# Scores of the state-space scan: sixteen 64x64 products a chunk become eight products with 64 rows and 128 columns

## The reference, cut to what matters

```python
def step(state, inp):
    x_t, b_t, c_t, dt_t = inp
    decay = jnp.exp(dt_t * a)[..., None, None]
    b_bar = dt_t[..., None] * b_t
    state = decay * state + b_bar[..., None] * x_t[:, :, None, :]
    y_t = jnp.einsum('bhn,bhnp->bhp', c_t, state)
    return (state, y_t)
```

## Time and profile before

| | before |
|---|---|
| median of three runs | 1252.74 us |
| the three runs | 1251.51, 1252.74, 1256.01 us |
| the profiled execution's own time | 1251.51 us |
| its span, first to last instruction | 1249.4 us |
| TensorE busy (PE) | 1233.5 us, 99% of the span |
| TensorE weight load busy (PEld) | 1029.7 us, 82% |
| VectorE, ScalarE, GpSimd busy | 923.6, 612.0, 775.0 us |
| granted TensorE clock | 1.000 |

### The profile page before, as it was taken

One profiled execution on the slowest core, in us unless ns is written; L12 is line 12 of the kernel. 1 busy time (PEld: TensorE's weight loads), 2 busy tenths in 40 slices (PEclk: granted clock), 3 DMA queues, 4 the chain that ended last, 5 costly groups with the idle time before them and its releaser, 6 DMA issues.

```text
span 1249.4 us, 28240 instructions
## 1 busy us (share of the span) xinstructions
PE 1233.5 (99%) x11183; PEld 1029.7 (82%) x11185; DVE 923.6 (74%) x1868; ACT 612.0 (49%) x1276; POOL 775.0 (62%) x660
## 2 busy tenths in 40 slices
PE   8999999999999999999999999999999999999999
PEld 4666678888888888888888887789989999899998
DVE  7999877777675677677766657897777766776676
ACT  6999974444434344433433334444344332554453
POOL 4889845345454476666766656566666754566773
PEclk9999999999999999999999999999999999999999
DMA  9799759353454444435434445574455544799995
GB/s 293 258 338 351 292 202 211 135 170 128 141 173 141 166 134 133 156 147 178 136 121 166 148 144 175 191 176 89 92 114 95 96 92 105 230 322 332 334 320 176
DMA packets 122211, 231.18 MB, mean 185 GB/s; under 512 B 19168, under 2 KB 85984, under 8 KB 113760
## 3 DMA queue, kind: packets, MB, share of 16 engines
q1 hardware_dynamic: 108928, 212.08, 50.5%
q0 software_dynamic: 12288, 17.05, 8.0%
q10 hardware_dynamic: 864, 0.24, 0.1%
HBM read 147.81 MB, written 81.53 MB: 184 GB/s over the span
## 4 chain that ended last, share of the span: by engine, by line
PE 76%; DVE 8%; ACT 4%; POOL 4%; DMA 3%; issue 3%; SPq 1%; POOLq 0%; another core or an unknown queue 0%; ACTq 0%; DVEq 0%
PE ps L1273 22%; PE ps L1613 9%; PE ps L1870 8%; PE ps L2104 7%; PE ps L2083 7%; PE ps L1398 4%; PE ps L1328 3%; PE ps L1410 2%; PE ps L1361 2%; PE ps L1378 2%; PE ps L1344 2%; DMA y_dram<-yb 2%; PE ps L693 2%; PE ps L641 1%; ACT decay L1240 1%
## 5 line engine op out<-in xcount | busy, mean ns | idle before, releaser
L1240 ACT ACTIVATE decay<-tap,ncum 128x128 f32<-128x128 f32 x344 | 105.4, 389 | 150.5 <-POOL tap L1153 150.5
L1798 POOL DMA_INDIRECT ffn_dram<-ob,idx x64 | 110.3, 1724 | 81.6 <-DVE ob L1717 67.8
L1071 DVE TENSOR_TENSOR yb<-ps,yb 128x256 f32<-128x256 f32 x128 | 48.4, 420 | 146.0 <-PE ps L1410 141.3
L1832 ACT ACTIVATE mid<-ps,b_up 128x512 f32<-128x512 f32 x96 | 65.9, 689 | 156.0 <-PE ps L1613 130.4
L1182 POOL TENSOR_SCALAR yb<-x,dcol 128x512 f32<-128x512 f32 x64 | 48.9, 764 | 129.9 <-DMA y_dram<-yb 95.3
L1159 POOL TENSOR_TENSOR x_lo<-x,x_hi 128x512 fp32r<-128x512 f32 x56 | 73.6, 1314 | 80.5 <-ACT x_hi L1226 80.4
L1170 POOL TENSOR_TENSOR c_dec<-cT,ecum_row 128x512 f32<-128x512 f32 x64 | 89.2, 1394 | 35.9 <-PE ps L1410 26.3
L1273 PE MATMUL ps<-x_hi,w_hi_b 128*128 128x512 f32 x240 | 99.6, 415 | 0.6 <-ACT bT L1230 0.6
L1273 PE MATMUL ps<-x_hi,w_hi_c 128*128 128x512 f32 x240 | 99.4, 414 | 0.0
L1959 POOL TENSOR_SCALAR yc<-yc,gn_scale,gn_shift 128x512 f32<-128x512 f32 x56 | 76.7, 1381 | 32.4 <-DMA yc<-y_dram 32.4
L1273 PE MATMUL ps<-x_lo,w_hi_b 128*128 128x512 f32 x240 | 94.4, 393 | 0.0
(11 more groups left out here) (313 smaller groups left out, 3948.0 us busy)
## 6 DMA issues: line engine op xcount, KB each, us to landing
tap<-cum_dram SPq DMA_DIRECT2D x43, 512.0 KB
x_dram<-x SPq DMA_DIRECT2D x16, 1024.0 KB, 5.7
x<-x_dram SPq DMA_DIRECT2D x16, 1024.0 KB, 5.6
ecum_row<-ecum_dram SPq DMA_DIRECT2D x128, 128.0 KB
y_dram<-yb SPq DMA_DIRECT2D x16, 1024.0 KB, 7.4
yc<-y_dram SPq DMA_DIRECT2D x16, 1024.0 KB, 6.8
cum_row<-cum_dram SPq DMA_DIRECT2D x21, 512.0 KB
rows_dram<-xn SPq DMA_DIRECT2D x16, 512.0 KB, 3.3
```

The costliest lines, as they stand in the source:

```text
L1240: n = nc.scalar.activation(decay[g % 2][:, h, :], cum_row[g % NR][:, h, :], ACT.Exp, bias=t.ncum[:, g, h:h + 1])
L1798: pool.indirect_dma_start(out=t.ffn_dram, out_offset=bass.IndirectOffsetOnAxis(ap=t.idx[:, e, h * HC + c:h * HC + c + 1], axis=0), in_=ob[ ...
```

## The change

Before, each head's 128x128 score matrix is made of two products: 64 weight columns of `bT` each, writing partitions 0 to 63 and 64 to 127 of the bank (`j` = 0, 1). With the two heads of a pair these are four products on four quarters of the array. After, each head's matrix is one product with all 128 weight columns, writing all 128 partitions; the two heads of a pair use the upper and the lower 64 rows of the array. The wait ahead of them, the banks, and the semaphore behind them stay.

```diff
             until(pe, mix_ready, 2 * g)
             for m in range(MT):
-                for j, a in ((0, 0), (1, 1), (1, 0), (0, 1)):
-                    r, rows = slice(a * HD, (a + 1) * HD), slice(j * HD, (j + 1) * HD)
-                    mm = pe.matmul(ps_g[a][rows, m * P:(m + 1) * P],
-                                   bT[b % 2][r, m, c * P + j * HD:c * P + (j + 1) * HD], cT[b % 2][r, m, cols],
+                for a in range(2):
+                    r = slice(a * HD, (a + 1) * HD)
+                    mm = pe.matmul(ps_g[a][:, m * P:(m + 1) * P], bT[b % 2][r, m, cols], cT[b % 2][r, m, cols],
                                    start=True, stop=True)
             mm.then_inc(g_ready, 1)
```

## The result

The change made the kernel slower: 1262.27 us (median of 4 runs, 1262.00 to 1262.38) against 1252.97 us (median of 4, 1251.51 to 1256.01). The ratio is 1.007, with a 95% interval of 1.0058 to 1.0083. Beside a later set of 12 runs of the kernel before (1252.69 us), five more runs of the changed one gave 1262.14 us and 1.0074 (1.0060 to 1.0088). So it costs 9.3 to 9.5 us. The forecast was +14.0, and its range held the time.

A forecast was written before the change was run, and what follows sets the result against it. TensorE was taken as the bound. Form change 6.1, first loads 6.7 and 0.2, later loads 1.5 made 14.5 us, less 0.5 for waits: +14.0, predicted as 1266.5 us, range 1254 to 1279.

The forecast's parts named there:

- The bound: In the scan TensorE sets the time; PE waited 2.9 us in all, so time added between chunks moves the end equally.
- Work: 0: In the scores, 32 matmuls become 16, still 8 waves of 128 columns, so fewer instructions gain 0.
- A new change of form: 0.10 us: Between L1410 (64*64) and the scores (64*128), leaving the form costs 0.10 us in 61 chunks: 6.1 us.
- The first load: 0.11 us: The scores' first weight load, 128 columns, stands bare: 0.11 us in 61 chunks, 6.7 us; 0.2 us in three others.
- later loads 0.112 us a wave: Later score loads nearly hide behind passes: a wave takes 0.112 us instead of 0.109, 1.5 us in 64 chunks.
- The stream: TensorE's added time in the scan from form change, bare loads and slower waves: 14.5 us before shrinking waits.
- Other engines: 0, and 0.5 us for the waits that shrink: Later scores delay nothing beyond TensorE, as VectorE's 2.5 us idle covers it; waits for x_dt shrink by 0.5 us.
- The loads of the halves side by side: In the scores, weight loads for upper and lower rows run together, not in turn, as L1328's 64-column loads did.
- the first rival: Score loads don't hide, by halves loading in turn or not under their own pass: +69, about 1322 us; chance 0.10.
- the half-free entry: Entering the scores costs only one of two parts, form change or bare first load: +6 to +8 us.
- the free entry: Going from 64*64 to 64*128 ahead of the scores empties nothing and the first load hides: +1.7, about 1254.5 us; chance 0.12.
- the exit that costs nothing: Leaving the scores for L1361 is free as both use all columns; with free entry -9, about 1243.5 us; chance 0.03.

The follow-up runs named there:

- The doubled kernels: Every score product computed twice, in the kernel before (1303.03 us against 1253.43, ratio 1.0396) and in the changed kernel (1317.07 us, ratio 1.0513).

## Why the prediction was right, and where a size was off

- *The bound.* TensorE is the bound: of 55.9 us of doubled work on it 49.6 came back, and once its waits were used up, 14.0 of 14.8. The step that said that time added between two chunks moves the end by as much holds only past the first few microseconds.
- *Work: 0.* Right. The wave took 0.109 us with four products of 64 columns in it and 0.112 with two of 128. Half the instructions bought nothing.
- *A new change of form: 0.10 us.* Right: 0.110 (488 to 598 ns), in 61 places. The pair of forms that no row had, 64*64 to 64*128, costs the same as the forecast's others (0.09 to 0.12), though only the columns change.
- *The first load: 0.11 us, later loads 0.112 us a wave.* The waves were 0.112. Bare load and way out together came to 0.198 us, where I had 0.11 + 0.12 = 0.23. So that sum was 0.03 too high in each chunk, 2 us in all. By the durations the bare load was 0.101 of it (373 - 272 ns), which leaves 0.097 for the way out; in the old form the way out was 0.111.
- *The stream.* Foretold 14.5 us, measured 13.5 in the two groups; another 0.008 us in the usual chunk lies outside them.
- *Other engines: 0, and 0.5 us for the waits that shrink.* This is the term that was mis-sized. It measured 4 us between the undoubled kernels, and some 6 are there to be filled. About 2.8 us of the 4 are waits that the two traces show as gone, and the rest is that the profiled execution of the kernel before was 1.2 to 1.9 us shorter than the medians. I had taken the 2.9 us of listed waits for all, and expected few of them to go. But a wait ahead of a matmul appears only as the part of it that outlasts the pipelined duration of the one before: 0.21 us shown for some 0.43 lost at 639 us. Starts of groups, compared with the usual chunk, show it in full. The trace of the changed kernel also spent 1.1 us less ahead of the scan and 1.2 us less behind it (449.6 us from the last scores on, against 450.8). In its second trace the scan began at 192.5 us, as before, and the part behind it took 450.6, so that was chance.
- *The loads of the halves side by side.* Right: the second wave begins 0.21 us after the first for both halves. That a half also loads under its own pass, the first rival's other question, is shown by the half alone, at 0.112 us a wave. The Trainium skill, TensorE: Matmul & The Clock Gate, The mechanism, has a list by which a load overlaps with running matmuls "only when row_grp differs". The run with one half behind the other disagrees with that sentence, at 0.112 us a wave on one row half. The same section also has loads pulled ahead of running matmuls when they go to the background weight buffer, and that the run would fit.
- *Rivals.* By the time alone the half-free entry would have been nearer than the forecast: its terms add up to 7.8 to 8.4 us (not 6 to 8, as I wrote), and 9.3 was measured. The starts decide: both parts are there, 0.110 us ahead of the scores and a bare load of 0.10 in them. So the free entry is out, and the half-free one with it (10.7 us of idle loads in 62 places). So is the exit that costs nothing: the scores' 1.092 us hold 0.894 of waves and 0.198 besides.

What stays open: why the waits of the kernel before differ from one execution to the next. The lists name ScalarE's copy of `bT` and GpSimd's `c_dec`; what makes these late three times in one execution and six times in another wasn't followed. The doubled kernels show that most of the waits go when TensorE is slower.

## What to carry to other kernels

On a stream bound by TensorE, count changes of form before you count instructions. In this kernel a change put 0.10 to 0.11 us behind the last wave, plus the first weight load, bare, at 0.05 us for 64 float32 columns and about 0.10 for 128; so products of a shape that matches their neighbours can be worth more than fewer, larger ones. If two row halves are to run together, issue their products alternately.

Read waits of a pipelined engine from the starts of groups, not from its idle time, and allow a few microseconds of them to swallow the first part of any added work.

## What the runs showed of the hardware that was not expected

With the products of one row half behind those of the other, TensorE began the second half's 0.55 us after the first half's and ran them side by side from there: 1.64 us for the scores, against 1.09 with the halves alternating and 1.99 for no overlap. By the starts, matmuls began out of the order of the program, the ninth beside the fifth.
